# Moving the row of maxima ahead of the exponential in a two-layer cross-attention kernel (ScalarE's order in a slot)

## The reference, cut to what matters

```python
def _mha(q, k, v, heads=HEADS):
    ...
    scores = jnp.einsum('bhqd,bhkd->bhqk', qh, kh) * jnp.asarray(d, q.dtype) ** (-0.5)
    probs = jax.nn.softmax(scores, axis=-1)
    out = jnp.einsum('bhqk,bhkd->bhqd', probs, vh)
    ...
# layer 0
hs = _mha(hidden_states @ Wq, enc @ Wk, enc @ Wv)
...
out = (hs + ca_hs2) @ Wout + b_out + residual
# layer 1: the same softmax attention with 20 heads over all 375 rows, @ Wo + bo, + residual
```

## Time and profile before

| | |
|---|---|
| median of 3 runs | 810.22 us (807.76 to 814.08) |
| the profiled execution's own time | 808.88 us |
| its span, first to last instruction | 807.1 us |
| busy: PE / PEld / DVE / ACT / POOL | 725.3 / 620.7 / 474.5 / 396.6 / 292.9 us |
| mean granted TensorE clock | 0.97 of full speed |
| chain that ended last, by engine | PE 59%, DMA 12%, DVE 11%, ACT 11%, issue 5% |
| transfers of mT issued by ACT | 32 (L563) and 80 (L566) |

### The profile page before, as it was taken

One profiled execution on the slowest core, in us unless ns is written; L12 is line 12 of the kernel. 1 busy time (PEld: TensorE's weight loads), 2 busy tenths in 40 slices (PEclk: granted clock), 3 DMA queues, 4 the chain that ended last, 5 costly groups with the idle time before them and its releaser, 6 DMA issues.

```text
span 807.1 us, 18167 instructions
## 1 busy us (share of the span) xinstructions
PE 725.3 (90%) x6920; PEld 620.7 (77%) x6920; DVE 474.5 (59%) x1027; ACT 396.6 (49%) x922; POOL 292.9 (36%) x401
## 2 busy tenths in 40 slices
PE   4989699999799999989899999999998899999885
PEld 3767588888688878878787887888787788878764
DVE  2543375756457575756657575766666475666662
ACT  2434355555455555545455555545555455544432
POOL 7536434423243433332343432423343242330300
PEclk9897899999999999999999999999999999999987
DMA  8326242432714253351814254251716225070500
GB/s 304 105 79 152 77 115 80 85 107 55 144 32 112 78 98 97 64 128 31 169 31 103 81 85 112 52 142 31 163 38 113 70 56 135 3 170 1 81 1 15
DMA packets 51907, 72.45 MB, mean 90 GB/s; under 512 B 11776, under 2 KB 43904, under 8 KB 51824
## 3 DMA queue, kind: packets, MB, share of 16 engines
q1 hardware_dynamic: 44784, 61.85, 31.4%
q0 software_dynamic: 6144, 9.25, 5.5%
q10 hardware_dynamic: 896, 0.20, 0.1%
HBM read 20.60 MB, written 4.26 MB: 31 GB/s over the span
## 4 chain that ended last, share of the span: by engine, by line
PE 59%; DMA 12%; DVE 11%; ACT 11%; issue 5%; ACTq 2%; SPq 0%; POOL 0%; DVEq 0%; POOLq 0%
PE bankX L973 24%; DMA q1T<-mT 10%; PE bankST L1161 7%; PE bankO L1193 6%; PE bankST L1155 5%; ACT arena L555 4%; DVE negmax L759 4%; PE bankS L1127 3%; ACT arena L573 3%; DVE q1T L815 2%; PE bankS L1124 2%; PE bankX L1093 2%; ACT q1T L644 2%; PE bankX L1073 1%; PE bankX L1101 1%
## 5 line engine op out<-in xcount | busy, mean ns | idle before, releaser
L759 DVE TENSOR_REDUCE negmax<-bankS 112x2 f32<-112x750 f32 (+1 forms) x224 | 208.7, 932 | 84.0 <-PE bankS L1127 51.1
L479 POOL DMA_DIRECT2D k_stack<-stage x192 | 96.6, 511 | 179.3 <-PE bankST L1155 166.0
L555 ACT ACTIVATE arena<-bankST 125x1344 f32<-125x1344 f32 x80 | 103.5, 1294 | 54.6 <-PE bankST L1161 54.6
L1193 PE MATMUL bankO<-arena,v 125*32 125x112 f32 (+2 forms) x2688 | 109.5, 267 | 5.9 <-ACT arena L555 4.6
L1193 PEld LDWEIGHTS bankO<-arena,v 125*32 125x32 f32 (+2 forms) x2688 | 82.8, 119 | 30.0 <-issue 15.2
L1127 PE MATMUL bankS<-k_stack,q1T 112*112 112x376 f32 x320 | 90.4, 364 | 3.1 <-DVE negmax L759 2.7
L1161 PE MATMUL bankST<-q1T,k_stack 112*125 112x224 f32 x480 | 68.9, 279 | 18.8 <-DMA q1T<-mT 18.6
L973 PE MATMUL bankX<-ctx_hi,WH 128*120 128x376 f32 (+2 forms) x192 | 71.7, 373 | 15.2 <-ACT arena L573 11.1
L459 POOL TENSOR_TENSOR x1b<-x,bias_sb 112x320 f32<-112x320 f32 x16 | 13.9, 870 | 185.1 <-DMA out<-x1b 158.7
L1161 PEld LDWEIGHTS bankST<-q1T,k_stack 112*125 112x125 f32 x480 | 61.5, 190 | 24.0 <-DMA q1T<-mT 23.7
L973 PE MATMUL bankX<-WH,ctx_hi 128*125 128x320 f32 x192 | 66.2, 345 | 1.1 <-ACT v L610 0.6
(11 more groups left out here) (138 smaller groups left out, 1549.7 us busy)
## 6 DMA issues: line engine op xcount, KB each, us to landing
k_stack<-stage SPq DMA_DIRECT2D x96, 176.2 KB
k_stack<-stage SPq DMA_DIRECT2D x192, 70.5 KB, 3.9
k_stack<-stage POOLq DMA_DIRECT2D x192, 47.0 KB, 3.3
ctx_raw<-in_ctxT SPq DMA_DIRECT2D x16, 376.0 KB, 3.0
k_stack<-stage SPq DMA_DIRECT2D x48, 117.5 KB
xp<-in_xpad SPq DMA_DIRECT2D x16, 224.0 KB, 4.0
x_raw<-in_xT SPq DMA_DIRECT2D x16, 168.0 KB, 2.3
out<-x1b SPq DMA_DIRECT2D x16, 140.0 KB, 3.6
```

The lines of the kernel that those rows point to most:

```text
L479: pool.dma_start(dst, src).then_inc(k1_stacked_pool[b % 2], 16)
L555: nc.scalar.activation(dst[0:KC], bankST[0:KC, :, 0:GROUP * SQ], ACT.Exp).then_inc(exp_done, 1)
L759: nc.vector.tensor_reduce(negmax[:, n % 2, 2 * pair:2 * pair + 2], bankS[0:SQ, :, 0:keys], axis=AX, op=ALU.max, negate=True).then_inc(max_ ...
L1193: last = nc.tensor.matmul(dst, v, src[0:keys, c, SQ * j:SQ * j + SQ], start=(c == 0), stop=(c == NKC - 1))
```

## The change

In ACT's walk through a slot, `place_m(before)` moves from behind the drains of phase 1 to ahead of `exps(late)`. Nothing is added or taken away: the same 112 transfers, the same exponentials and drains, the same waits. The programs of PE, DVE, POOL and SP are the same, instruction for instruction.

```diff
                     for u in units_of(t, i, 0):
                         unit(*u)
+                    if before:
+                        place_m(before)
                     if late:
                         exps(late)
                     for u in units_of(t, i, 1):
                         unit(*u)
-                    if before:
-                        place_m(before)
                     if i == 3 and t < B:
                         round_p3(t)
```

## The result

The changed kernel takes 913.56 us in the median of 4 runs (912.59 to 921.75), the kernel before 808.99 beside it: 1.134 times the time, with a 95% interval of 1.126 to 1.143. The forecast was 886 with a range of 842 to 908: the right side, 5.6 us beyond the range. The profiled execution took 912.97 us, with a span of 911.2, so 104.1 us more span than before.

What follows compares the result with a forecast made beforehand. PE was taken to bound the kernel, with almost no slack behind ACT's late drains. Slot costs of 84.8 us less 5.4 and 2 of saved waits gave 77.4 on 808.9, forecast 886 us, range 842 to 908.

Steps and rivals of the forecast that it cites:

- The price ahead of the exponential: On ACT, the exponential starts 0.04 + 0.64 us after DVE's copy of the maxima, as the transfer's issue holds the queue.
- The rival of a free queue: On ACT, the issue does not hold the queue, so the exponential starts 0.05 us after it begins: 841 us, chance 0.12.
- The slots: Lateness per slot: 1.04 us in 0 and 5, 1.03 in 1, 1.54 in 6, none in 2 and 4.
- Slot 3: In slot 3, the pair of exponentials ends later and the attend starts 0.94 us late, 15 times: 14.1 us.
- The cover: In slot 2, PE's 0.80 us wait for the small exponentials ahead of K1_2 hides the late attend: cost 0.
- What it gives back: PE's waits for the transfer shrink by 5.4 us for four in slot 6 and 2 for twelve in slot 5.
- the sum: Lateness over all slots, 84.8 us, less 5.4 and 2 of saved transfer waits: 77.4 us added to the profiled 808.9.
- the clock as a rival: TensorE's clock halves in PE's new gaps, 1.5 us a stretch in each of 15 iterations: 22 us more, 908, chance 0.13.
- PE's busy sum: On PE, the changed kernel's profile would show its own busy sum staying near 725 us.
- behind it: After the loop, 1.5 us for slots 5 and 6 of t = 15, and 4.0 for four slots in the tail.
- The rival on the other side: The exponential's later start lies in slack and PE's 18.6 us of transfer waits go: 790 us, chance 0.03.
- the rule by itself: Issuing the transfer early and waiting late puts its fixed cost beside work; alone it gives the 790 us case.

Runs made afterwards that it cites:

- e2: Against the kernel before: ACT waits for DVE's copy ahead of the exponential, but the transfer is issued in its old place; 841.8 us, ratio 1.042.
- e3: Against the changed kernel: each transfer cut into two of half the size, both ahead of the exponential; 1025.8 us.
- e1: Against the kernel before: the transfer placed behind the exponential but ahead of the drains of phase 1; 804.36 us, ratio 0.996.
- e10: Against the kernel before: the change in slot 3 alone; 815.47 us, ratio 1.017.
- e9: Against the kernel before: the change in all slots but slot 2; 899.75 us, ratio 1.123.
- e4: Against the changed kernel: small idle matmuls added where PE waits, 7 ahead of out0, 12 ahead of q1, 6 ahead of the attend in slots 0 to 3; 911.85 us.
- e5: Against the changed kernel: fewer idle matmuls, 5 ahead of out0, 7 ahead of q1, and 4, 4, 2, 4 ahead of the attend in slots 0 to 3; 895.57 us.
- e8: Against the kernel before: the transfer behind the exponential and ahead of the drains of phase 1, but slot 6 left as it was; 799.72 us, ratio 0.9915.
- e7: Against the kernel before: the change in slots 2 and 4 alone; 800.29 us, ratio 0.993.

## Why the prediction was right in kind and too low

*The price ahead of the exponential* (forecast 0.68 from copy to exponential, measured 0.71): right. The single place of the earlier trace rows gave 0.64 for the held queue; the changed kernel shows 0.68. The rival of a free queue is out by e2 and e3, and e1 rules out that the earlier transfer itself does harm.

*The slots*: in their medians, 1, 2, 4, 5, 6 and 0 came within 0.07 us of the working. *Slot 3* was mis-sized: 0.94 forecast, 1.17 measured, 3.2 us in the loop. Its own steps have 1.01 (e10); the other 0.17 is slot 2's, which I had put at nothing. The wait of the earlier trace rows did cover PE, whose K1_2 now starts without a wait. It did not cover ACT and DVE. The changed kernel, an iteration earlier than above, from slot 2 into slot 3:

```profile
473.69 0.39 DVE L776 COPY o0T<-bankO 128x224 f32<-128x224 f32 x1 [0.85 <-PE bankO L1193]
...
474.72 0.35 ACT L573 ACTIVATE arena<-bankX,negmax 112x112 f32<-112x112 f32 x1 [0.40 <-DVE negmax L823]
...
476.56 0.54 DVE L795 TENSOR_TENSOR stage<-bankX,stage 64x376 fp32r<-64x376 f32 x1 [0.47 <-ACT stage L597]
476.57 0.26 PE L1140 MATMUL bankO<-cst,negmax 112*4 112x112 f32 x1
477.03 0.25 DVE L765 CAST mT<-bankO 4x112 fp32r<-4x112 f32 x1
```

The late attend makes DVE's second maximum of the small scores late, so the second half of the small exponentials waits for it (0.40); K1_2's drain on ACT and then on DVE follow, and DVE copies the maxima only behind that, 0.46 after the transpose where it was 0.30 (the copy at 474.50 in the earlier trace rows, the transpose at 474.20). With slot 2 left alone it is 0.30 again in every iteration (e9). The cover was read on PE, and the lateness went round it through the two other queues.

*What it gives back*: 7.4 us forecast, 9.2 measured (18.6 to 9.4). The four waits in slot 6 are gone, as forecast (6.0 us, 5.4 forecast); the twelve in slot 5 went from 12.6 to 9.4, where I had 2 less. That slot 4's interval gains from lateness in slot 3 (e10) was not in the sum.

*The failing step: the clock as a rival beside the sum and not a term in it.* I gave 0.13 to "the clock falls in the new gaps", as an alternative, because each gap was shorter than the 1.89 of the earlier trace rows, and let the likeliest case run at full clock. The changed kernel shows 12 stretches at half clock in the loop where before has 2, the one above behind waits of 0.58 and 0.59 us in slot 1 and 0.73 in slot 2; the longest in the 20 us ahead of them was 1.68, also below 1.89. A wait of 1.7 to 2.0 ahead of q1 stands in each of the fourteen iterations, and the clock fell in slot 6 in four of them only. So the size of a single gap was the wrong bound. Filling the gaps brings the full clock back (e4, e5), and that is worth 11.6 us, twice the 5.6 by which the time left the range. The rival's price of 1.5 us for one stretch was right (9.57 against 8.09 in slot 6); its count, one in each iteration, was near the 12 found, and the sum had none. PE's busy sum shows it too: 749.2 us where I expected near 725, as matmuls at half clock take longer.

*The whole, in spans*: from the first transpose of iteration 1 to that of iteration 15 the changed kernel takes 728.3 us and before 638.8, so 89.5 more, where the sum had 71.0. Of the 18.5 missing, 11.6 are the clock, 3.2 slot 3 and 2.4 the 0.04 or 0.05 in four slots; less what was gained beyond the forecast, some 3 stay unexplained; the nine falls priced above have 12 us by themselves, so a part of the 3 may be clock too. Ahead of the loop 4.0 us were lost, where I had 0; behind it 10.5, where I had 6.4, with about 8 us more at half clock than before. The 4.0 ahead are no effect of the change that the runs show, and count as chance: the first transpose of iteration 1 lies at 96.5 us in before and in e1, at 93.4 in e8, 94.5 in e5, 101.2 in e2 and 103.1 in e7, by whether PE is at half clock until 26 to 28 us (the first four) or until 42 (the last two), where no transfer of maxima has been issued yet and all of these run the same program. In the changed kernel it was 42, in e5 26: that is the 6 us between them. Why it differs is open. Without the 4.0 the time would still lie 1.6 us beyond the range.

*The rival on the other side* (the transfer's wait is what counts, 790 us) named a true gain with the wrong place for it: e8 and e7 get 0.7 to 0.9% with transfers issued early where little waits behind them. The rule of the Trainium skill (DMA: Bandwidth & Descriptors, Rules for kernel authors) is to issue early and wait late. Those two kernels agree with it; the changed kernel, which also issues earlier, takes 913.56 us where the rule by itself points below 808.99, since it does not speak of what stands behind the issue in the issuing engine's queue.

## What to carry to other kernels

The issue of a transfer is an instruction of the engine's queue: ask what stands right behind it, and put it behind an instruction that runs longer than the issue, not ahead of one that others wait for. A step that is moved ahead brings its wait with it, and everything behind it inherits that wait; follow the lateness through every queue that the late engine feeds, not only through the one that seems covered. Costs of single slots need not add up: lateness in one can take up a wait in the next. And when a sum adds many short idle gaps to TensorE, put the clock into the sum.

## What the hardware showed that was not expected

An issue of a 1.8 KB transfer holds ScalarE's queue for 0.58 us, and the next instruction starts 0.68 after its start; issued beside a running exponential it leaves the whole time as it was (804.36 us in e1), and costs 0.34 us in slot 6, where V0_1's drain waits behind it. TensorE's granted clock fell to half (1.2 of 2.4 GHz) again and again in a loop whose PE was busy for 84% (611.58 of 729 us) and whose longest wait was 2.0 us. Added matmuls in the gaps, with PE then busy for 94% (673.40 of 717), kept it up nearly throughout: adding work made the loop 11.6 us shorter.
